# Reordering the last image's inner points, and halving one output's copy and add, in a two-layer convolution kernel

## The chip, the cores and the metric

The kernel runs on one NeuronCore of a Trainium2 chip. The metric is device time in microseconds; the runs of the kernel before gave 274.39, 275.0 and 276.09 us.

## What is computed

A batch of 16 images of 128 channels and 32 x 32 pixels passes through two residual layers. Each normalises in groups of four channels and convolves with 3 x 3 taps. The first layer mixes four expert kernels per image with a routing weight; the second uses the signs of its weights.

```python
pooled = jnp.mean(x, axis=(2, 3))
routing = jax.nn.sigmoid(pooled @ w_route.T + b_route)
y = conv(x, w_experts)                         # four experts, 3 x 3, pad 1
out = jnp.einsum('beohw,be->bohw', y, routing)
out = silu(out * inv + shift)                  # batch norm's scale and offset
...
x = x + _L0_conv_ref(_gn(x), ...)
x = x + _L1_conv_ref(_gn(x), W)                # conv with sign(W), 3 x 3, pad 1
```

## The kernel before

All 16 images stay in SBUF in the tile X, one column block of 1024 pixels each (128 channels on the partitions). The five engines run one hand-written instruction list each, and semaphores order them against one another; each engine's list is strictly in order. A loop over t runs from 1 to 16: in round t TensorE (PE) multiplies the first layer of image t in a transformed (Winograd) form, where rows are taken in tiles of four and each tile becomes six points (M1, M2, P1, P2, P0, PINF), and then the second layer of image t - 1 directly, as nine taps in two parts. The input is split into hi and lo, both f16, since the signs are exact in f16; so a half image (16 rows, one PSUM bank of pc) takes 9 products with hi and 9 with lo (sign_half, L569).

The second layer's output of an image goes from pc through ScalarE (ACT, evacuate, L945) into ev, and GpSimd (POOL, add_output, L430) adds it by a DMA that accumulates in DRAM, onto the first layer's output which SyncE (SP) has stored there (L403). POOL also takes the reciprocal root of each variance (power, L421).

The last image, 15, has no round after it, so its second layer is done in another way, behind the loop. Its first 24 rows go through the six points with f16 hi and lo parts; its last 8 rows are direct products (last_direct, L628). The names, in the order of each engine's list:

- VectorE (DVE): residual_last (L1254) adds the first layer, centre_last, last_rows_of_points (L1296, L1300), last_transform (L1308 and L1309 for the inner points M1 to P2, L1312 for the end points P0 and PINF; each raises last_v_ready, up to 5), last_low_parts (L1323 three times, for the pairs M1 and M2, P1 and P2, P0 and PINF; L1327 for the last rows), last_inverse (sums, L1336, to X, L1354) and last_outputs (L1363 twice, for the rows that P0 and PINF give).
- ACT: last_mean, last_variance (L749 to L760), variance (L808), last_hi (L923 three times, L925 for the last rows; the third waits for last_v_ready 5), evacuate of image 14 (L945), last_copy_minus (L931, which copies the bank pb into minus), last_direct_out (L936, with its own store, L939).
- PE: behind image 14's hi products come its lo products, among them the last image's residual (L617) and group variance (L494); then sign_conv_last, in this order: last_pair for pb with hi and lo, for pa with hi and lo (L606), last_direct with hi and lo (L628), last_pair for pe_ with hi and lo. A hi part waits for last_hi_ready, a lo part for last_lo_ready.
- SP: the store of the last image's 24 rows (L406) waits for both of DVE's L1363; then SP waits for the stores (stored) and for the adds (out_added).

last_inverse waits for pa (last_m_ready 2) and for ACT's minus. The three pairs each have one PSUM bank, pb, pa and pe_. The order of sign_conv_last and of ACT's tail is:

```python
for n in range(2):
    last_pair(0, n)
    last_pair(1, n)
last_direct(0)
...
last_hi()
evacuate(B - 2)
last_copy_minus()
last_direct_out()
```

Of the kernel before, what the change touches and what calls it, by code (L numbers as in the profile page):

```python
# [10 lines left out]
ALU = mybir.AluOpType  # L11
# [3 lines left out]
E, K = 4, 3  # L15
HW = H * W
# [47 lines left out]
def build(nc, x, w_experts, w_sign, params, out):  # L64
# [6 lines left out]
    with ExitStack() as ctx:  # L71
# [175 lines left out]
        h_stored = [sem(f"h_stored{i}") for i in range(B - LATE)]  # L247
        out_added = [sem("out_added0"), sem("out_added1")]
        out_ready = sem("out_ready")
        stored = sem("stored")  # L250
# [113 lines left out]


        def columns_to(c):

            return sum(cols(k)[1] - cols(k)[0] for k in range(1, c + 1))
# [12 lines left out]
        def _(sp):  # L381
# [26 lines left out]
            for p in range(2):  # L408
                sp.wait_ge(out_added[p], 16 * ((B - LATE + 1 - p) // 2))

        @block.gpsimd
        def _(pool):
# [14 lines left out]
            def add_output(i):  # L427
                pool.wait_ge(h_stored[i], 16)
                pool.wait_ge(evacuated, i + 1)
                g.dma_start(out_v[i, :, :], ev[i % 2][:], accum_op=ALU.add).then_inc(out_added[i % 2], 16)  # L430

            g.memset(nhalf[:], -0.5).then_inc(zeroed, 1)
            g.memset(ones16[:], 1.0).then_inc(zeroed, 1)
# [17 lines left out]
            for t in range(1, B + 1):  # L451
                power(t + LAG - 1)
                if 0 <= t - 2 < B - LATE:
                    add_output(t - 2)
                if ND <= t < B and t not in DVE_RESIDUAL:
                    residual(t)

        @block.tensor
        def _(pe):
# [125 lines left out]
            def last_pair(part, n):  # L585

                r = rank(B)
                bank, points = ((pb, (M1, M2)), (pa, (P1, P2)), (pe_, (P0, PINF)))[n]  # L590
                if part == 0:
                    pe.wait_ge(last_hi_ready, n + 1)
                    if n == 0:
                        pe.wait_ge(sign_points_ready, 4)
                        pe.wait_ge(minus_ready, r)
                    elif n == 1:
                        pe.wait_ge(sums_ready, 2 * r)
                    else:
                        pe.wait_ge(y_ready, 4 * r + 2)
                else:  # L600
                    pe.wait_ge(last_lo_ready, n + 1)
                for j, k in enumerate(points):
                    weights = ws[:, (k - P0) * 2 * KCO:((k - P0) * 2 + 1) * KCO] if k >= P0 else wpoint[:, k, :]
                    for m, kx in enumerate(KX_ORDER):
                        c0, c1 = reach(kx, 0, W, W)
                        mm = mm_(bank[:, 0:LAST_TILES, j, c0:c1], weights[:, kx * C:(kx + 1) * C],  # L606
                                 last_points((hi, lo)[part])[:, :, k, c0 + kx - 1:c1 + kx - 1],
                                 start=(part == j == m == 0), stop=(part == j == 1 and m == K - 1))
                if part == 1:
                    mm.then_inc(last_m_ready, 1)  # L610

# [22 lines left out]
            def sign_conv_last():  # L634
                for n in range(2):
                    last_pair(0, n)
                    last_pair(1, n)
                last_direct(0)
                last_direct(1)
                last_pair(0, 2)  # L640
                last_pair(1, 2)

# [27 lines left out]
            for t in range(1, B + 1):  # L670
# [13 lines left out]
                elif t == B - 1:  # L684
# [7 lines left out]
                    sign_half(t - 1, 1, 0, TAP_ORDER[5:])  # L692
                    sign_half(t - 1, 1, 1)
                else:
# [8 lines left out]
        def _(act):  # L703
# [38 lines left out]
            def last_variance():  # L742
# [3 lines left out]
                for half in range(2):  # L746
# [4 lines left out]
                               accum_out=(var[:, c, MID:MID + 1], last_var[:])[half]).then_inc(var_mid_ready, 1)  # L751
                    if half == 0:
                        squares(c)
                        act.wait_ge(dev2_ready, c)
                        act.wait_ge(var_mid_ready, i + 1)
                        activation(last_spread[:], dev2[:, c, MID:MID + 1], ACT.Identity, bias=var[:, c, MID:MID + 1],
                                   scale=float(HW)).then_inc(last_spread_ready, 1)
                act.wait_ge(last_spread_ready, 1)
# [182 lines left out]
            def evacuate(i):  # L941
# [3 lines left out]
                activation(ev[i % 2][:], flat(pc[:]), ACT.Copy, scale=1.0 / ACT_SCALE).then_inc(evacuated, 1)  # L945

            for q in (1, 3):
                act.dma_start(quarter(q), x_quarters[0, q, :, :]).then_inc(x_quarter_loaded[q], 16)
# [75 lines left out]
            last_hi()  # L1024
            evacuate(B - 2)
            last_copy_minus()
            last_direct_out()

        @block.vector
        def _(dve):  # L1030
# [271 lines left out]

            def last_transform():
                er, fr, vi = e_rows[:, 0:LAST_TILES], f_rows[:, 0:LAST_TILES], V[0][:, 0:LAST_TILES]
                dve.wait_ge(last_e_ready, 1)
                dve.wait_ge(last_f_ready, 1)
                for k, op, scale in ((M1, ALU.subtract, -2.0), (P1, ALU.add, 2.0)):
                    v.tensor_tensor(vi[:, :, k, :], er[:, :, 2, :], er[:, :, 1, :], op).then_inc(last_v_ready, 1)  # L1308
                    v.scalar_tensor_tensor(out=vi[:, :, k + 1, :], in0=fr[:, :, 0, :], scalar=scale,  # L1309
                                           in1=fr[:, :, 1, :], op0=ALU.mult, op1=ALU.add).then_inc(last_v_ready, 1)  # L1310
                ew = er.rearrange("p t k w -> p t (k w)")
# [3 lines left out]
            def last_low_parts():  # L1315
                c = CHAINS - 1
                dve.wait_ge(rstd_ready, c + 1)

                dve.wait_ge(sign_points_ready, 4)
                for n, k in enumerate((M1, P1, P0)):  # L1320
                    dve.wait_ge(last_hi_ready, n + 1)
                    dve.wait_ge(last_v_ready, (2, 4, 5)[n])
                    v.scalar_tensor_tensor(out=last_points(lo)[:, :, k:k + 2, :], in0=V[0][:, 0:LAST_TILES, k:k + 2, :],  # L1323
                                           scalar=rstd[:, c, MID:MID + 1], in1=last_points(hi)[:, :, k:k + 2, :],
                                           op0=ALU.mult, op1=ALU.subtract).then_inc(last_lo_ready, 1)
                dve.wait_ge(last_hi_ready, 4)
# [30 lines left out]
            def last_outputs():  # L1357
                dve.wait_ge(inner_added, 1)
                dve.wait_ge(last_m_ready, 4)
                rows = img(B - 1).rearrange("p (t k w) -> p t k w", k=TROWS, w=W)  # L1360
                for k, row, scale in ((0, 0, K_ZERO), (1, 3, K_INF)):
                    part = rows[:, 0:LAST_TILES, row, :]
                    v.scalar_tensor_tensor(out=part, in0=pe_[:, 0:LAST_TILES, k, :],  # L1363
                                           scalar=scale * INVERSE_SCALE / LAST_SCALE, in1=part,
# [100 lines left out]
```

## Time and profile before

| what | us |
|---|---|
| runs: lowest, median, highest | 274.39, 275.0, 276.09 |
| span of the profiled execution, first to last instruction | 276.8 |
| PE busy | 267.2 |
| DVE busy | 255.8 |
| ACT busy | 219.8 |
| POOL busy | 54.4 |

Of the profiled execution the span is what the profile gives; it is 1.8 us longer than the median of the runs. Times in the rows are microseconds from the start of the span. A line of a timeline or of a chain gives the start, the duration, the engine, the line of the kernel and the operation, what it writes and reads, and how many instructions are merged (x9); in brackets stands how long the engine was idle before it and who ended that. The ends of PE's products are modelled, and a product's record overlaps the next one's; the distance of two starts is the better price.

### The profile page before, as it was taken

What the parts mean: (1) busy time and instruction counts of PE and PEld (TensorE: products, weight loads), DVE (VectorE), ACT (ScalarE), POOL (GpSimd) and SP (SyncE); (2) the same over time, 40 slices, a digit from 0 to 9 for tenths busy, and PEclk for the clock granted to TensorE, in tenths of its full rate; (3) what the DMA queues carried; (4) which work ended last, traced back from release to release, by engine and by line L of the source; (5) the groups of instructions that cost most, each with busy time, mean ns of one, the idle gap of its engine ahead of it and who ended that gap; (6) DMA issues with size and microseconds to landing.
All of it is one profiled execution on the core that took longest, in us unless ns stands there. A gap on an engine that the chain in (4) does not pass through costs nothing.

```text
span 276.8 us, 4115 instructions
## 1 busy us (share of the span) xinstructions
PE 267.2 (97%) x1336; PEld 183.2 (66%) x1336; DVE 255.8 (92%) x466; ACT 219.8 (79%) x450; POOL 54.4 (20%) x63
## 2 busy tenths in 40 slices
PE   7699989999999999999999999999999999999993
PEld 7444764857667584857667584857667584857663
DVE  5679979999999999999999999999999999996885
ACT  2458789897979989798989989798989987745870
POOL 3001011311203141311303141311314141210110
PEclk9779999999999999999999999999999999999999
DMA  7988953163554536264454436254554437273507
GB/s 216 394 316 290 322 182 76 78 114 114 78 153 60 99 91 127 82 97 134 76 152 62 94 88 129 89 94 133 78 153 57 95 90 133 85 123 107 76 2 152
DMA packets 11253, 35.20 MB, mean 127 GB/s; under 512 B 1248, under 2 KB 3424, under 8 KB 11232
## 3 DMA queue, kind: packets, MB, share of 16 engines
q0 software_dynamic: 4176, 15.21, 33.0%
q1 hardware_dynamic: 6624, 19.34, 18.9%
q10 hardware_dynamic: 432, 0.39, 0.4%
q8 instruction: 11, 0.18, 0.3%
q14 instruction: 10, 0.08, 0.1%
HBM read 11.34 MB, written 16.25 MB: 100 GB/s over the span
## 4 chain that ended last, share of the span: by engine, by line
PE 91%; DMA 3%; DVE 2%; ACT 1%; issue 1%; SPq 1%; POOL 0%; DVEq 0%; ACTq 0%
PE pc L569 41%; PE pa L534 14%; PE pb L534 14%; PE pe_ L534 13%; PE pd L524 6%; DMA we<-w_experts 3%; PE ps L504 1%; PE ps L508 1%; DVE U L1129 0%; PE pa L606 0%; POOL rstd L421 0%; PE pb L606 0%; DVE X L1354 0%; ACT hi L906 0%; SPq L389 0%
## 5 line engine op out<-in xcount | busy, mean ns | idle before, releaser
L1139 DVE SCALAR_TENSOR_TENSOR U<-we,route,U 128x1152 f32<-128x1152 f32 x45 | 63.6, 1413 | 0.6
L569 PE MATMUL pc<-hi,ws 128*128 128x496 f16 (+3 forms) x270 | 59.8, 375 | 0.8 <-ACT hi L906 0.8
L569 PE MATMUL pc<-lo,ws 128*128 128x496 f16 (+3 forms) x270 | 59.7, 375 | 0.0
L421 POOL TENSOR_TENSOR rstd<-ve,nhalf 128x2 f32<-128x2 f32 (+1 forms) x19 | 26.7, 1407 | 139.4 <-ACT ve L821 113.2
L569 PEld LDWEIGHTS pc<-hi,ws 128*128 128x128 f16 x270 | 26.4, 98 | 30.3 <-issue 1.2
L569 PEld LDWEIGHTS pc<-lo,ws 128*128 128x128 f16 x270 | 26.5, 102 | 27.8
L534 PE MATMUL pa<-V,UM 128*128 128x256 f32 (+1 forms) x180 | 41.7, 381 | 0.0
L534 PE MATMUL pb<-V,UM 128*128 128x256 f32 (+1 forms) x180 | 40.7, 376 | 0.1
L534 PE MATMUL pe_<-V,U 128*128 128x256 f32 (+1 forms) x180 | 40.6, 375 | 0.0
L534 PEld LDWEIGHTS pb<-V,UM 128*128 128x128 f32 x180 | 34.1, 190 | 5.4 <-issue 0.6
L534 PEld LDWEIGHTS pe_<-V,U 128*128 128x128 f32 x180 | 34.1, 190 | 3.8
L534 PEld LDWEIGHTS pa<-V,UM 128*128 128x128 f32 x180 | 33.1, 190 | 3.3
L425 POOL DMA_DIRECT2D X<-y x14 | 12.4, 883 | 65.6 <-ACT y L891 65.6
L729 ACT ACTIVATE junk_mid<-X,stats 128x1024 f32<-128x1024 f32 x15 | 17.2, 1148 | 9.4 <-DMA X<-y 9.4
L906 ACT ACTIVATE hi<-X,nbias,rstd 128x1024 f16<-128x1024 f32 (+2 forms) x16 | 18.9, 1187 | 0.5
L863 ACT ACTIVATE U<-we,route 128x1152 f32<-128x1152 f32 x15 | 18.8, 1256 | 0.5
L845 ACT ACTIVATE xn<-X,nbias,rstd 128x1024 f32<-128x1024 f32 (+1 forms) x16 | 19.2, 1200 | 0.0
L524 PE MATMUL pd<-xn,U 128*128 128x496 f32 (+3 forms) x36 | 18.2, 653 | 0.3 <-DVE U L1129 0.3
L913 ACT ACTIVATE hn<-X,nbias,rstd 128x1024 f32<-128x1024 f32 x15 | 18.4, 1229 | 0.0
L1261 DVE TENSOR_TENSOR lo<-hn,hi 128x1024 f16<-128x1024 f32 x15 | 18.3, 1221 | 0.0
L1170 DVE SCALAR_TENSOR_TENSOR e_rows<-xn 128x1024 f32<-128x1024 f32 x15 | 18.2, 1216 | 0.0
L891 ACT ACTIVATE y<-y,bn_shift,bn_tiles 128x1024 f32<-128x1024 f32 x14 | 17.2, 1230 | 1.2 <-DVE y L1240 1.2
(165 smaller groups left out, 396.1 us busy)
## 6 DMA issues: line engine op xcount, KB each, us to landing
X<-x SPq DMA_DIRECT2D x15, 512.0 KB, 5.1
out<-X SPq DMA_DIRECT2D x15, 512.0 KB, 2.6
out<-ev POOLq DMA_DIRECT2D x15, 512.0 KB, 5.5
X<-y POOLq DMA_DIRECT2D x14, 512.0 KB, 4.5
we<-w_experts SPq DMA_DIRECT2D x3, 768.0 KB, 10.0
ws_raw<-w_sign SPq DMA_DIRECT2D x1, 576.0 KB, 12.5
out<-X SPq DMA_DIRECT2D x1, 384.0 KB, 2.8
X<-x SPq DMA_DIRECT2D x2, 128.0 KB, 2.8
```

What stands on the lines that cost most here:

```text
L421: g.tensor_tensor(rstd[:, c, a:b], ve[:, c, a:b], nhalf[:, a:b], ALU.pow).then_inc(rstd_ready, 1)
L524: mm = mm_(rows[:, r0 - half * (H // 2):r1 - half * (H // 2), c0:c1], U[i % RING][:, slot, kx * C:(kx + 1) * C], xn[i % RING][:, r0 + ky:r ...
L534: mm = mm_(bank[:, :, j, c0:c1], weights[:, kx * C:(kx + 1) * C], V[t % 2][:, :, k, c0 + kx - 1:c1 + kx - 1], start=(n == 0), stop=(n == K ...
L569: mm = mm_(rows[:, r0 - first // W:r1 - first // W, c0:c1], ws[:, tap * C:(tap + 1) * C], plane((hi, lo)[part], i)[:, r0 + ky - 1:r1 + ky ...
L729: activation(junk["mid"][:], img(i), ACT.Square, bias=nm(c, MID), accum_out=var[:, c, MID:MID + 1]).then_inc(var_mid_ready, 1)
L845: activation(xn[i % RING][:, 1 + first:1 + last, :], img(i).rearrange("p (h w) -> p h w", h=H)[:, first:last, :], ACT.Identity, bias=nbias ...
L863: activation(flat(U[i % RING][:]), flat(we[:, 0, :, :]), ACT.Copy, scale=route[:, i, 0:1]).then_inc(mix_first, 1)
L906: activation(plane(hi, i)[:, first:last, :], img(i).rearrange("p (h w) -> p h w", h=H)[:, first:last, :], ACT.Identity, bias=nbias[:, c, M ...
L913: activation(hn[:], img(i), ACT.Identity, bias=nbias[:, c, MID:MID + 1], scale=rstd[:, c, MID:MID + 1]).then_inc(hn_ready, 1)
L1139: v.scalar_tensor_tensor(out=flat(U[i % RING][:]), in0=flat(we[:, e, :, :]), scalar=route[:, i, e:e + 1], in1=flat(U[i % RING][:]), op0=AL ...
L1170: v.scalar_tensor_tensor(out=flat3(e_rows[:]), in0=flat(xn[i % RING][:, 0:H, :]), scalar=-4.0, in1=flat(xn[i % RING][:, 2:2 + H, :]), op0= ...
L1261: v.tensor_tensor(lo[i % 2][:, 0:HW], hn[:], hi[i % 2][:, 0:HW], ALU.subtract).then_inc(lo_ready, 1)
```

## The change

Image 14's lo products of the second half are split: four taps stay, two go between the hi and lo parts of the first inner pair (pb), and three go behind the second inner pair (pa). The end points come last as before, but in a function of their own (last_ends) that does P0 with hi and lo and then PINF with hi and lo, PINF into the unused half of pd, so that DVE's last_outputs has a wait for each.

On DVE the transform and the low parts are cut up: inner points, low part of M1 and M2, low part of P1 and P2, end points, low part of P0 and PINF, low part of the last rows. On ACT the squares and the spread of the last variance come behind both halves' squares instead of between them; the evacuation of image 14 is done in halves, the first ahead of last_copy_minus, the second behind it. POOL adds each half with a DMA of its own, behind its loop; SP waits for both. last_hi on ACT is as before.

```diff
@@ sync
-                sp.wait_ge(out_added[p], 16 * ((B - LATE + 1 - p) // 2))
+                sp.wait_ge(out_added[p], 16 * ((B - LATE - p) // 2))
+                sp.wait_ge(half_added[p], 16)
@@ gpsimd
+            def add_output_half(i, half):
+                part = slice(half * BANK, (half + 1) * BANK)
+                pool.wait_ge(h_stored[i], 16)
+                pool.wait_ge(evacuated, i + half + 1)
+                g.dma_start(out_v[i, :, part], ev[i % 2][:, part], accum_op=ALU.add).then_inc(half_added[half], 16)
...
-                if 0 <= t - 2 < B - LATE:
+                if 0 <= t - 2 < B - LATE - 1:
                     add_output(t - 2)
...
+            for half in range(2):
+                add_output_half(B - 2, half)
@@ tensor
+            def last_ends():
+                r = rank(B)
+                pe.wait_ge(last_hi_ready, 3)
+                pe.wait_ge(y_ready, 4 * r + 2)
+                pe.wait_ge(silu_ready, 1)
+                for j, k in enumerate((P0, PINF)):
+                    weights = ws[:, j * 2 * KCO:(j * 2 + 1) * KCO]
+                    for part in range(2):
+                        if j == 0 and part == 1:
+                            pe.wait_ge(last_lo_ready, 3)
+                        for m, kx in enumerate(KX_ORDER):
+                            c0, c1 = reach(kx, 0, W, W)
+                            mm = mm_(last_end(j)[:, :, c0:c1], weights[:, kx * C:(kx + 1) * C],
+                                     last_points((hi, lo)[part])[:, :, k, c0 + kx - 1:c1 + kx - 1],
+                                     start=(part == m == 0), stop=(part == 1 and m == K - 1))
+                    mm.then_inc(last_m_ready, 1)
...
             def sign_conv_last():
-                for n in range(2):
-                    last_pair(0, n)
-                    last_pair(1, n)
+                i = B - 2
+                last_pair(0, 0)
+                sign_half(i, 1, 1, TAP_ORDER[4:6])
+                last_pair(1, 0)
+                last_pair(0, 1)
+                last_pair(1, 1)
+                sign_half(i, 1, 1, TAP_ORDER[6:])
                 last_direct(0)
                 last_direct(1)
-                last_pair(0, 2)
-                last_pair(1, 2)
+                last_ends()
...
-                    sign_half(t - 1, 1, 1)
+                    sign_half(t - 1, 1, 1, TAP_ORDER[:4])
@@ scalar
-                    if half == 0:
-                        squares(c)
...
+                squares(c)
+                act.wait_ge(dev2_ready, c)
+                act.wait_ge(var_mid_ready, i + 1)
+                activation(last_spread[:], dev2[:, c, MID:MID + 1], ACT.Identity, bias=var[:, c, MID:MID + 1],
+                           scale=float(HW)).then_inc(last_spread_ready, 1)
...
+            def evacuate_half(i, half):
+                act.wait_ge(conv_ready, 2 * i + half + 1)
+                act.wait_ge(out_added[i % 2], 16 * (i // 2))
+                activation(ev[i % 2][:, half * BANK:(half + 1) * BANK], pc[:, half, :], ACT.Copy,
+                           scale=1.0 / ACT_SCALE).then_inc(evacuated, 1)
...
             last_hi()
-            evacuate(B - 2)
+            evacuate_half(B - 2, 0)
             last_copy_minus()
+            evacuate_half(B - 2, 1)
             last_direct_out()
@@ vector
-                dve.wait_ge(last_m_ready, 4)
...
                 for k, row, scale in ((0, 0, K_ZERO), (1, 3, K_INF)):
+                    dve.wait_ge(last_m_ready, 4 + k)
...
-                    v.scalar_tensor_tensor(out=part, in0=pe_[:, 0:LAST_TILES, k, :],
+                    v.scalar_tensor_tensor(out=part, in0=last_end(k),
...
-            last_transform()
-            last_low_parts()
+            last_transform_pairs()
+            last_low_pair(0)
+            last_low_pair(1)
+            last_transform_ends()
+            last_low_pair(2)
+            last_low_rest()
             last_inverse()
             last_outputs()
```

## Rows read from the trace of the kernel before

**Rows 1.** The page's first part: span, and busy time of an engine
```profile
span 276.8 us, 4115 instructions
PE 267.2 (97%) x1336; PEld 183.2 (66%) x1336; DVE 255.8 (92%) x466; ACT 219.8 (79%) x450; POOL 54.4 (20%) x63
```

**Rows 2.** The chain that ended last, its end: start, us, what
```profile
269.84 0.56 DVE sums L1336
...
272.96 0.36 DVE X L1363
```

**Rows 3.** Timeline of PE from 264.6: start, us, line, operation
```profile
264.83 2.92 PE L569 MATMUL pc<-lo,ws 128*128 128x465 f16 x13
267.58 0.66 PE L606 MATMUL pb<-hi,wpoint 128*128 128x192 f16 x6
...
269.07 0.66 PE L606 MATMUL pa<-lo,wpoint 128*128 128x192 f16 x6
269.57 1.11 PE L628 MATMUL pd<-hi,ws 128*128 128x256 f16 x9
...
271.46 0.66 PE L606 MATMUL pe_<-hi,ws 128*128 128x192 f16 x6
271.96 0.66 PE L606 MATMUL pe_<-lo,ws 128*128 128x192 f16 x6
```

**Rows 4.** Timeline of ACT from 264.9
```profile
266.16 1.62 ACT L923 ACTIVATE hi<-V,rstd 128x384 f16<-128x384 f32 x3 [0.89 <-POOL rstd L421]
267.69 0.52 ACT L925 ACTIVATE hi<-xn,rstd 128x288 f16<-128x288 f32 x1
268.11 1.00 ACT L945 ACTIVATE ev<-pc 128x1024 f32<-128x1024 f32 x1
269.02 0.47 ACT L931 ACTIVATE minus<-pb 128x384 f32<-128x384 f32 x1
```

**Rows 5.** Timeline of DVE from 266.1
```profile
266.15 0.55 DVE L1312 TENSOR_TENSOR V<-e_rows 128x384 f32<-128x384 f32 x1
266.98 1.68 DVE L1323 SCALAR_TENSOR_TENSOR lo<-V,rstd,hi 128x384 f16<-128x384 f32 x3 [0.28 <-ACT hi L923]
268.57 0.51 DVE L1327 SCALAR_TENSOR_TENSOR lo<-xn,rstd,hi 128x288 f16<-128x288 f32 x1
...
272.96 0.62 DVE L1363 SCALAR_TENSOR_TENSOR X<-pe_,X 128x192 f32<-128x192 f32 x2
```

**Rows 6.** Timeline of POOL, its last two adds and the root between them
```profile
256.88 0.89 POOL L430 DMA_DIRECT2D out<-ev  x1 [1.30 <-ACT ev L945]
265.36 0.76 POOL L421 TENSOR_TENSOR rstd<-ve,nhalf 128x1 f32<-128x1 f32 x1 [7.59 <-ACT ve L808]
269.66 0.89 POOL L430 DMA_DIRECT2D out<-ev  x1 [3.53 <-ACT ev L945]
```

**Rows 7.** SyncE's waits from 260 (us in total, times, longest), and its last store
```profile
SPq L71 <- DMA out<-X: 1.2, 1, 1.2
SPq L409 <- DMA out<-ev: 1.2, 1, 1.2
...
273.61 0.33 SPq L406 DMA_DIRECT2D out<-X  x1
```

**Rows 8.** The page's DMA issues: KB each, us from issue to landing
```profile
out<-X SPq DMA_DIRECT2D x15, 512.0 KB, 2.6
out<-ev POOLq DMA_DIRECT2D x15, 512.0 KB, 5.5
...
out<-X SPq DMA_DIRECT2D x1, 384.0 KB, 2.8
```

**Rows 9.** ACT's groups by shape: copies out of PSUM, busy us, mean ns
```profile
L945 ACT ACTIVATE ev<-pc 128x1024 f32<-128x1024 f32 x15 | 15.5, 1031 | 0.0
...
L880 ACT ACTIVATE minus<-pb 128x512 f32<-128x512 f32 x15 | 8.9, 595 | 0.0
```

**Rows 10.** DMA from 256.8 to 263.0: busy tenths in 40 slices of 0.155 us
```profile
DMA  0000000004900009597996999999996000000000
```

More of the change, by code:

```diff
@@ L248, in build @@
         out_added = [sem("out_added0"), sem("out_added1")]
+        half_added = [sem("half_added0"), sem("half_added1")]
         out_ready = sem("out_ready")
@@ L363, in last_rest, with last_end @@
             return part[(B - 1) % 2][:, n:n + LAST_REST * W].rearrange("p (h w) -> p h w", w=W)
+        def last_end(j):
+            bank = flat3(pe_[:]) if j == 0 else pd[:, 1, :]
+            return bank[:, 0:LAST_TILES * W].rearrange("p (t w) -> p t w", w=W)
         def columns_to(c):
@@ L589, in last_pair @@
                 r = rank(B)
-                bank, points = ((pb, (M1, M2)), (pa, (P1, P2)), (pe_, (P0, PINF)))[n]
+                bank, points = ((pb, (M1, M2)), (pa, (P1, P2)))[n]
                 if part == 0:
@@ L595, in last_pair @@
                         pe.wait_ge(minus_ready, r)
-                    elif n == 1:
+                    else:
                         pe.wait_ge(sums_ready, 2 * r)
-                    else:
-                        pe.wait_ge(y_ready, 4 * r + 2)
                 else:
@@ L602, in last_pair @@
                 for j, k in enumerate(points):
-                    weights = ws[:, (k - P0) * 2 * KCO:((k - P0) * 2 + 1) * KCO] if k >= P0 else wpoint[:, k, :]
                     for m, kx in enumerate(KX_ORDER):
                         c0, c1 = reach(kx, 0, W, W)
-                        mm = mm_(bank[:, 0:LAST_TILES, j, c0:c1], weights[:, kx * C:(kx + 1) * C],
+                        mm = mm_(bank[:, 0:LAST_TILES, j, c0:c1], wpoint[:, k, kx * C:(kx + 1) * C],
                                  last_points((hi, lo)[part])[:, :, k, c0 + kx - 1:c1 + kx - 1],
@@ L751, in last_variance @@
                                accum_out=(var[:, c, MID:MID + 1], last_var[:])[half]).then_inc(var_mid_ready, 1)
-                    if half == 0:
-                        squares(c)
[L754 to L757, printed above, removed]
+                squares(c)
[3 more added lines that the diff above has]
+                           scale=float(HW)).then_inc(last_spread_ready, 1)
                 act.wait_ge(last_spread_ready, 1)
@@ L1301, in last_rows_of_points, with last_transform_pairs @@
                                 rows(0)[:, :, W:3 * W], ALU.subtract).then_inc(last_f_ready, 1)
-            def last_transform():
+            def last_transform_pairs():
                 er, fr, vi = e_rows[:, 0:LAST_TILES], f_rows[:, 0:LAST_TILES], V[0][:, 0:LAST_TILES]
@@ L1310, in last_transform, with last_transform_ends @@
                                            in1=fr[:, :, 1, :], op0=ALU.mult, op1=ALU.add).then_inc(last_v_ready, 1)
+            def last_transform_ends():
+                er, vi = e_rows[:, 0:LAST_TILES], V[0][:, 0:LAST_TILES]
                 ew = er.rearrange("p t k w -> p t (k w)")
@@ L1313, in last_transform, with last_low_pair, last_low_rest @@
                                 ew[:, :, 2 * W:4 * W], ew[:, :, 0:2 * W], ALU.subtract).then_inc(last_v_ready, 1)
-            def last_low_parts():
-                c = CHAINS - 1
+            def last_low_pair(n):
+                c, k = CHAINS - 1, (M1, P1, P0)[n]
                 dve.wait_ge(rstd_ready, c + 1)
                 dve.wait_ge(sign_points_ready, 4)
[L1320 to L1325, printed above, removed]
+                dve.wait_ge(last_hi_ready, n + 1)
+                dve.wait_ge(last_v_ready, (2, 4, 5)[n])
+                v.scalar_tensor_tensor(out=last_points(lo)[:, :, k:k + 2, :], in0=V[0][:, 0:LAST_TILES, k:k + 2, :],
+                                       scalar=rstd[:, c, MID:MID + 1], in1=last_points(hi)[:, :, k:k + 2, :],
+                                       op0=ALU.mult, op1=ALU.subtract).then_inc(last_lo_ready, 1)
+            def last_low_rest():
+                c = CHAINS - 1
                 dve.wait_ge(last_hi_ready, 4)
```

## The prediction

> **What bounds the kernel now.** I read the page first: TensorE is busy for 267.2 of the 276.8 us of the span [rows 1], so nearly everything up to the last image is set by PE's own queue, and the change leaves that part alone. It only reorders work after about 262 us. So the second view is the chain that ended last, of the last 15 us [rows 2]: PE runs without a gap through image 14's products and the inner pairs of the last image (pb, pa), and from there VectorE carries the end: the sums at 269.84, and the last writes into X from 272.96. The third view is the timeline of each engine over that stretch [rows 3, 4, 5, 6], read for what each queue does next. The last is SyncE's waits and the DMA landings [rows 7, 8]: SP waits 1.2 us for image 14's added output, and after it another 1.2 us for the store of the last image, so the store is what ends the span. It is issued at 273.61 and lands 2.8 us later, 276.41; the span closes 0.4 us behind that. Hence what moves the end is the moment at which DVE finishes X, 273.58 (272.96 + 0.62 [rows 5]), and, some 1.2 us of slack behind it, image 14's add (issued 269.66, landing 5.5 later: 275.2).
>
> What starts DVE's last chain? Its sums need three things: pa (PE, last pair issued at 269.07 and ended 269.73 [rows 3]), minus (ACT, 269.02 + 0.47 = 269.49 [rows 4]) and DVE itself being through with its low parts (268.57 + 0.51 = 269.08 [rows 5]). Today pa is last, with ACT only 0.24 us ahead of it.
>
> **PE's part of the change.** Thirteen products of image 14 take from 264.83 to 267.58 [rows 3], 2.75/13 = 0.212 us each. Eight now stand ahead of the first pair, two between its hi and lo parts, three behind pa. PE reaches the first pair at 264.83 + 8 x 0.212 = 266.52. But that pair needs ACT's first hi: it starts at 266.16 behind POOL's rstd (265.36 + 0.76 = 266.12 [rows 6]) and takes 0.60 (three in 1.62 us [rows 4], started 0.51 apart), so to 266.76. DVE, which waits for the same hi, starts at 266.98 [rows 5]; I take a value between, 266.92, so PE stands for 0.40 us. From there: pb hi 0.50 us (four groups of six from 267.58 to 269.57 [rows 3]), two products 0.42, pb lo, pa hi and pa lo 0.50 each: the last group starts at 268.84 instead of 269.07. Five products fewer ahead of pa would be 1.06 us; two still lie ahead, which takes 0.42 off, and the stall 0.40: pa is earlier by only 0.23 us. Behind it PE does the three products (0.64), the direct rows (0.94 + 0.95 [rows 3]) and the end points, and is through with issuing at 268.84 + 0.50 + 0.64 + 1.89 + 1.0 = 272.87, against 272.46 now. That 0.4 us costs nothing as long as DVE comes to the end points later than that; it does, below.
>
> **DVE's and ACT's part.** The transform of the end points (0.55 us at 266.15) now runs in time in which DVE would else wait for ACT's first hi: its idle time ahead of 266.98 is 0.28 us [rows 5]. The change puts it behind the second low part. The low parts gain nothing by that: the first waits for the first hi in either order, so it starts at 266.98 and the second 0.54 later (three in 1.68), and the transform runs from 268.05 to 268.60 instead of from 266.15 to 266.70. But ACT's third hi waits for that transform (last_v_ready 5), and that function is as before: ACT's queue is in order, so it stands from 267.28, when its second hi is done, to about 268.65. Behind it on ACT are the third hi (to 269.25), the rest's hi (0.52, to 269.68), now the copy of half an output, and only then minus. Starts on ACT follow each other 0.09 us inside the previous record (267.69 + 0.52 against 268.11 [rows 4]). The half copy of 512 columns is priced by the rows of 512 and 1024 columns out of PSUM, 0.60 and 1.03 us [rows 9]; I take 0.58: it runs from 269.58 to 270.15. Minus starts at 270.06 and ends at 270.53, where it ended at 269.49. With the 0.22 us from hi's end to DVE's start, the sums start at 270.75 instead of 269.84: **0.91 us later**. Halving the copy gives back 0.4 us of what the queue lost (a whole copy ahead would have been 1.03); the copy of the other half stands behind minus and needs conv_ready, at 270.1.
>
> Bounds of this term: with no hand-over time at all minus would be at hand at 270.45. But DVE itself isn't free before: its third low part waits for the third hi (269.25 + 0.22), takes 0.54, and the rest's low part 0.48 to the next start, so 270.49, or +0.65. With 0.2 us at each of the two hand-overs (DVE to ACT, ACT to DVE) it is +1.1. So +0.65 to +1.1, and I take 0.9.
>
> From the sums to the end of X DVE has the same instructions: 3.74 us [rows 2, 5], so 274.49. The two reads of the end points now lie in two banks and have a wait each; since DVE comes to them at 273.87 and PE issued its last group's end well before (272.87, with a fill of 0.2), both waits are met and the split is worth nothing. Without that cover it would save at most one group, 0.5 us. The store is issued at 274.52 and lands 2.8 later [rows 8] at 277.3.
>
> **The variance's reorder.** ACT's squares and spread move behind the second half's square. The same five instructions follow one another, the last one starting at about 264.2 as before; PE's group variance is issued behind the residual product and waits for it in either order. Zero, give or take 0.1, which would shift everything behind it alike.
>
> **The halved add.** POOL issues behind ACT's copy with 0.55 us of hand-over (269.11 to 269.66 [rows 4, 6]) and 0.89 an issue. Half 0: copy ended 270.15, issued 270.70. Half 1: copy from 270.44 to 271.0, issued 271.55 to 271.6. How long half an add takes no row shows. Whole ones land in 5.5 us [rows 8]; in the add that ran alone, issued at 256.88 [rows 6], the engines' busy stretch lies at 259.1 to 261.6 (slices 15 to 30 of 0.155 us [rows 10]), so 2.2 us ahead of the data, 2.5 of data, the rest completion. If data goes by bytes, half 1 moves from about 274.0 to 275.6 and lands at 276; if it goes by rows (as many rows, half as long), the two halves take 2.5 to 3.1 each behind one another from 273.0, to 278 or 279.2, and land with 0.3 more. SP's plain stores don't settle it, since of their landing little is data: 512 KB took 2.6 us and 384 KB 2.8 [rows 8]. I take nearer to the bytes, since with 16 engines busy through the whole stretch it is more likely the data than the count that fills it: half 1 lands between 276 and 277, under the store's 277.3. The Trainium skill (DMA: Bandwidth & Descriptors, Anatomy of one DMA) speaks against such a split: a DMA from GpSimd has about 2.0 us that doesn't scale, and only the rest goes by bytes at 436 GB/s. By it half an add would be an estimated 0.6 us shorter than a whole, landing at 276.5; no row here shows halves, and the sum stands without it.
>
> **Sum.** The end goes from 276.41 + 0.4 to 277.3 + 0.4 = 277.7 in the profiled execution, +0.9 us on 276.8. The median of the runs shown is 275.0, 1.8 below that execution; the same 0.9 on it gives **275.9**.
>
> **The rivals.**
> A, the forecast: ACT's queue is held by the late transform; +0.65 to +1.1, 275.6 to 276.1.
> B, faster: PE's pa stays what the sums wait for, and its 0.23 us is gained: 274.8. It decides if minus is at hand by 269.5, which takes a third hi that starts no later than about 267.6. For it speaks that pa is last today; against it that the third hi can't start ahead of the transform's end, which is at 268.6 by the order on DVE. If the first hi came 0.4 us sooner, B would be worth 0.6.
> C, slower still: the halves' adds go by rows and end the span. Half 1 at 278.3 to 279.5 instead of the store's 277.3 gives +1.9 to +3.1: 276.9 to 278.1. It decides once half an add lands more than 5.7 us after its issue at 271.6. For it: the DMA engines are already busy nearly throughout while one add moves [rows 10]; the store would share the engines with it. Against it: the traffic is the same in bytes.
> D, nothing to see: gains and losses under 0.3 us, because another instruction on ACT gives way (say the hand-overs are shorter than I took): 275.0.
>
> **How the numbers follow.** A 0.65, B 0.08, C 0.15, D 0.12. The runs of before spread from 274.39 to 276.09, so a median may sit half a microsecond off any case. The range reaches from B and D's lower side to the lower part of C: 274.6 to 277.2; A's own is 275.3 to 276.5. About 1%, 2.75 us, is what a measurement of this kernel can tell from no change. Over 1% slower needs the upper end of C, 277.75: 0.05. Over 1% faster has no case, 0.02 for what I don't see. The rest, 0.93, is within 1%.
>
> **What would show it.** PE idle for some 0.4 us ahead of its first pair, released by ACT's hi; ACT idle for some 1.4 us ahead of the third hi, released by DVE's last transform; DVE's sums released by ACT's minus at about 270.75 instead of by pa; the last X at 274.5; SP's last wait still for the store. The forecast is wrong if the sums start before 269.9, or if SP's last long wait is for the second half's add.

## The result

The changed kernel takes 276.41 us (median of 22 runs, 275.24 to 279.9), the kernel before 275.0 beside it. The ratio, from which the slow executions of both kernels are left out, is 1.0045 (95% interval 1.0028 to 1.0063), some 1.2 us slower; the medians of all runs differ by 1.4. The forecast was 275.9, 0.9 us slower.

The two profiled executions can't be compared by their spans, 276.8 and 274.9: the one of before ran the second and third of its 40 slices at a lower granted clock (digit 7, a mix of TensorE's 1.2 and 2.4 GHz levels), the one of after at 2.4 GHz throughout (9 tenths or more in every slice), which the page's second part shows (before, then after):

```profile
PEclk9779999999999999999999999999999999999999
```
```profile
PEclk9999999999999999999999999999999999999999
```

A run's time lies 1.8 us above its span (276.73 for the 274.9), so the 276.8 of before belongs to an execution some 3.6 us above the median of 275.0, not 1.8; the forecast only adds a difference to that median, so its number doesn't hang on this. All tails below are measured from one instruction that is the same in every kernel, PE's last group mean, which starts at 262.14 in the profile before and at 258.44 in the one after (timeline of PE, two products each). The profiles of e3, e7, e8 and e11 dip in the same two slices, ahead of the mean and so outside every tail.

```profile
262.14 0.38 PE L485 MATMUL ps<-stats,gmat 128*128 128x1 f32 x2
```
```profile
258.44 0.38 PE L500 MATMUL ps<-stats,gmat 128*128 128x1 f32 x2
```

After it, the timelines of the changed kernel read (start, us, line, tile; in brackets the idle time before and who ended it), first PE's products ahead of the first pair, that pair's hi part and pa's last group, then ACT, then DVE, then POOL and SP:

```profile
261.24 1.88 PE L584 MATMUL pc<-lo,ws 128*128 128x465 f16 x8
263.13 0.67 PE L618 MATMUL pb<-hi,wpoint 128*128 128x192 f16 x6
...
265.06 0.66 PE L618 MATMUL pa<-lo,wpoint 128*128 128x192 f16 x6
```
```profile
262.46 1.12 ACT L955 ACTIVATE hi<-V,rstd 128x384 f16<-128x384 f32 x2 [0.78 <-POOL rstd L428]
264.93 0.61 ACT L955 ACTIVATE hi<-V,rstd 128x384 f16<-128x384 f32 x1 [1.36 <-DVE V L1354]
265.45 0.52 ACT L957 ACTIVATE hi<-xn,rstd 128x288 f16<-128x288 f32 x1
265.88 0.57 ACT L982 ACTIVATE ev<-pc 128x512 f32<-128x512 f32 x1
266.36 0.47 ACT L963 ACTIVATE minus<-pb 128x384 f32<-128x384 f32 x1
```
```profile
263.28 1.15 DVE L1364 SCALAR_TENSOR_TENSOR lo<-V,rstd,hi 128x384 f16<-128x384 f32 x2 [0.74 <-ACT hi L955]
264.35 0.55 DVE L1354 TENSOR_TENSOR V<-e_rows 128x384 f32<-128x384 f32 x1
265.75 0.62 DVE L1364 SCALAR_TENSOR_TENSOR lo<-V,rstd,hi 128x384 f16<-128x384 f32 x1 [0.85 <-ACT hi L955]
266.28 0.51 DVE L1371 SCALAR_TENSOR_TENSOR lo<-xn,rstd,hi 128x288 f16<-128x288 f32 x1
266.86 0.56 DVE L1380 TENSOR_TENSOR sums<-pa,minus 128x384 f32<-128x384 f32 x1
...
270.26 0.35 DVE L1407 SCALAR_TENSOR_TENSOR X<-pd,X 128x192 f32<-128x192 f32 x1
```
```profile
267.00 1.79 POOL L443 DMA_DIRECT2D out<-ev  x2 [4.58 <-ACT ev L982]
```
```profile
270.64 0.33 SPq L412 DMA_DIRECT2D out<-X  x1
```

Against [rows 4], where ACT's three hi follow one another without a gap, ACT now stands 1.36 us ahead of the third, until DVE's transform of the end points (L1354) is done. Minus ends at 266.83, 8.39 us after the group mean, where it ended 7.35 after it (269.49). Against [rows 2], the sums start 8.42 instead of 7.70 us after the mean: 0.72 later, and the store is issued 12.20 instead of 11.47 after it [rows 7]. That is the forecast's mechanism, by two ways at once: the sums come 0.03 us behind minus, and 0.07 us behind DVE's own last low part (266.28 + 0.51 = 266.79), which the late third hi holds up just as much. But the store also lands later (DMA issues of the end of the span, KB each, us from issue to landing; then SP's waits in us):

```profile
out<-ev POOLq DMA_DIRECT2D x2, 256.0 KB, 4.8
out<-X SPq DMA_DIRECT2D x1, 384.0 KB, 3.7
```
```profile
SPq L416 <- DMA out<-ev: 2.4, 1, 2.4
SPq L71 <- DMA out<-X: 0.9, 1, 0.9
```

The store took 2.8 us [rows 8] and now takes 3.7. The forecast's sum had no such term.

### The profile page after: what moved, and what is told of

Read it like the earlier page. It is cut to its first block, busy times and chain, and to the rows that moved or that the text cites. A ratio compares the mean times of both kernels' runs of the same rounds, so it can differ in the third digit from the quotient of the medians.

```text
span 274.9 us, 4122 instructions
## 1 busy us (share of the span) xinstructions
PE 265.0 (96%) x1336; PEld 181.6 (66%) x1336; DVE 256.1 (93%) x466; ACT 219.9 (80%) x451; POOL 55.5 (20%) x64
## 4 chain that ended last, share of the span: by engine, by line
PE 90%; DMA 2%; DVE 2%; ACT 2%; issue 1%; POOL 1%; SPq 1%; DVEq 0%; ACTq 0%
PE pc L584 41%; PE pa L549 14%; PE pb L549 14%; PE pe_ L549 13%; PE pd L539 6%; DMA we<-w_experts 2%; PE ps L519 1%; POOL rstd L428 1%; PE ps L523 1%; DVE U L1168 0%; DVE X L1398 0%; DVE lo L1364 0%; ACT hi L938 0%; SPq L395 0%; ACT hi L955 0%
## 5 line engine op out<-in xcount | busy, mean ns | idle before, releaser
L539 PE MATMUL pd<-xn,U 128*128 128x496 f32 (+3 forms) x36 | 15.9, 586 | 1.1 <-DVE U L1168 1.1
```

What stands on the lines that cost most here:

```text
L539: mm = mm_(rows[:, r0 - half * (H // 2):r1 - half * (H // 2), c0:c1], U[i % RING][:, slot, kx * C:(kx + 1) * C], xn[i % RING][:, r0 + ky:r ...
```

## The experiments

Theory 1: ACT's queue, held up by the late transform, delays minus and the sums. Theory 2: the add of image 14 comes so late that the last store is held up by it. The rival of 2 is that two DMAs in place of one do it. Theory 3, made after e1 to e7, widens 2 to the kernel before: wherever an add is late, the last store lands 1.0 to 1.2 us after the last add has landed, and alone 2.3 us after its issue. All results, in us after PE's last group mean, each from the run's own profile; the adds' landing is issue plus the time to landing; "closes" is the end of the span; the ratio of times is against the kernel before, with its interval:

| kernel | sums | store issued | last add issued | last add landed | store takes | closes | ratio |
|---|---|---|---|---|---|---|---|
| before | 7.70 | 11.47 | 7.52 | 13.0 | 2.8 | 14.66 | |
| after | 8.42 | 12.20 | 9.46 | 15.0 | 3.7 | 16.46 | 1.0045 (1.0028 to 1.0063) |
| e1 ends early | 7.39 | 11.20 | 9.07 | 12.9 | 2.9 | 14.54 | 0.9996 (0.9963 to 1.0028) |
| e2 before, ends late | 8.85 | 12.62 | 8.99 | 14.3 | 2.9 | 15.92 | 1.0051 (1.0014 to 1.0088) |
| e3 no add of 14 | 8.42 | 12.19 | none | | 2.3 | 14.92 | 1.0001 (0.9966 to 1.0035) |
| e4 before, halves | 7.70 | 11.47 | 8.16 | 13.0 | 2.8 | 14.64 | 0.9993 (0.9960 to 1.0026) |
| e5 one add | 8.43 | 12.20 | 9.18 | 15.0 | 4.0 | 16.67 | 1.0125 (1.0081 to 1.0168) |
| e6 hi hi lo lo | 7.09 | 10.90 | 8.77 | 13.7 | 3.8 | 15.16 | 1.0007 (0.9979 to 1.0036) |
| e7 variance back | 8.43 | 12.20 | 9.4 | 14.8 | 3.6 | 16.35 | one execution |
| e8 half first | 7.70 | 11.47 | 8.16 | 12.0 | 2.3 | 14.18 | 0.9967 (0.9928 to 1.0005) |
| e9 before, no add of 14 | 7.70 | 11.47 | none | | 2.3 | 14.18 | 0.9969 (0.9933 to 1.0006) |
| e10 before, late add | 7.70 | 11.48 | 9.56 | 15.9 | 5.3 | 17.32 | 1.0093 (1.0056 to 1.0131) |
| e11 both | 7.17 | 10.98 | 8.85 | 12.9 | 3.2 | 14.53 | 0.9993 (0.9973 to 1.0013) |

**e1: DVE's order alone undone.**

```diff
             last_transform_pairs()
+            last_transform_ends()
             last_low_pair(0)
             last_low_pair(1)
-            last_transform_ends()
             last_low_pair(2)
```

> The changed kernel with one thing undone: DVE does the transform of the end points ahead of the first low part again. Theory 1 (ACT's queue, held by that transform, delays minus and with it DVE's sums): the 1.4 us gap ahead of ACT's third hi goes, the sums start 7.4 to 7.8 us after PE's last group mean (before 7.7, changed 8.4), and the time falls by 0.7 to 1.2 us, to 275.1 to 275.6. Theory 2 (the halved add, which runs beside the last store, carries the loss): the sums come earlier but the store still lands 3.5 us or more after its issue and the time stays at 276.0 or above.

ACT's gap is gone, minus is copied 1.5 us sooner, and the sums wait for pa again (timelines of ACT and DVE):

```profile
262.48 1.62 ACT L955 ACTIVATE hi<-V,rstd 128x384 f16<-128x384 f32 x3 [0.77 <-POOL rstd L428]
...
264.91 0.47 ACT L963 ACTIVATE minus<-pb 128x384 f32<-128x384 f32 x1
```
```profile
265.85 0.56 DVE L1380 TENSOR_TENSOR sums<-pa,minus 128x384 f32<-128x384 f32 x1 [0.44 <-PE pa L618]
```

The sums start 7.39 us after the mean, 1.03 sooner than in the changed kernel and 0.31 sooner than before: PE's reorder does give the sums what it promises, once ACT isn't held. The time is that of the kernel before (the interval allows 0.28%, 0.8 us, above it) and the span closes 0.12 us sooner, so undoing this one order takes the loss away. It takes away both its parts, since ACT's queue held the halves' copies as well as minus: the store took 2.9 us, which theory 2 as I had put it did not expect; the half copied first was added 1.5 us earlier here, and its packets were nearly through when the second one's began.

**e2: the kernel before with DVE's order alone changed.**

```diff
                 for n, k in enumerate((M1, P1, P0)):
+                    if n == 2:
+                        last_transform_ends()
                     dve.wait_ge(last_hi_ready, n + 1)
...
-            last_transform()
+            last_transform_pairs()
             last_low_parts()
```

last_transform is cut into two functions for it, with the same instructions.

> The kernel before with only DVE's order changed: the transform of the end points stands behind the second low part. Theory 1: ACT idles about 1.4 us ahead of the third hi, and here a whole copy of image 14 stands ahead of minus, so the sums start about 1.4 us later than before (9.1 after PE's last group mean) and the time rises by 1.2 to 1.6 us, to 276.2 to 276.6. Rival: DVE's order is harmless, the sums stay at 7.7 and the time at 275.0 to 275.3.

ACT stands 1.36 us ahead of its third hi here too, and DVE's sums wait for minus:

```profile
264.37 0.61 ACT L923 ACTIVATE hi<-V,rstd 128x384 f16<-128x384 f32 x1 [1.36 <-DVE V L1315]
```
```profile
266.73 0.56 DVE L1341 TENSOR_TENSOR sums<-pa,minus 128x384 f32<-128x384 f32 x1 [0.67 <-ACT minus L931]
```

DVE's own low parts are through at 266.06 here. Minus ends at 266.70, so the hand-over from ACT takes 0.03 us. The sums are 1.15 us later than before, a little less than expected, and the ratio 1.0051 is 1.4 us. The loss follows the order on DVE without PE's change. The ACT copy ahead of minus is a whole one here, and it stands behind the same gap, so the add is late as well (issued 8.99, 1.47 later than before), about as much as the store (1.15).

**e3 and e9: no add of image 14, in the changed kernel and in the kernel before.**

```diff
-            for half in range(2):
-                add_output_half(B - 2, half)
...
-                sp.wait_ge(half_added[p], 16)
```

That is e3, in which both halves are still copied. e9 ends POOL's loop of adds one image earlier, and SP waits for one add less:

```diff
-                if 0 <= t - 2 < B - LATE:
+                if 0 <= t - 2 < B - LATE - 1:
                     add_output(t - 2)
```

> The changed kernel without image 14's add (both halves are copied but not added, so that image lacks its second layer). Theory 2 (the store of the last image shares the DMA engines with the halves' adds): the store lands 2.5 to 2.9 us after its issue instead of 3.7, and the time falls by 0.7 to 1.0 us to 275.4 to 275.7. Rival: the store's 3.7 us come from its own queue or from ACT's small store beside it; it stays at 3.5 to 3.9 and the time at 276.2 to 276.5.

> The kernel before without image 14's add (that image lacks its second layer). Theory 3: also in the kernel before it is the add that holds up the store, so the store lands in 2.2 to 2.4 us instead of 2.8 and the time falls by 0.4 to 0.6 us. Rival (in the kernel before the add is out of the store's way): 2.7 to 2.9 us, and no difference in time.

Without the add the store lands 2.3 us after its issue in both (DMA issues, the same line in e3 and e9):

```profile
out<-X SPq DMA_DIRECT2D x1, 384.0 KB, 2.3
```

So in the changed kernel the add costs the store 1.4 us, and in the kernel before 0.5. Theory 3's 2.2 to 2.4 (e9) holds; theory 2's 2.5 to 2.9 (e3) was too high, and its rival's 3.5 to 3.9 is out. ACT's small store (128 KB) takes 1.7 us in both, against 3.4 in the kernel before and 4.9 in the changed one, so the add holds that one up too. With no add in either, the changed kernel's span closes 0.74 us later (14.92 against 14.18): that is DVE's chain alone, and the other 1.06 of the 1.80 between the two kernels comes only with the add. In time, e3 falls to that of the kernel before, a little more than the 0.7 to 1.0 us expected; e9's ratio 0.9969 has an interval that reaches to 1.0006, so its half microsecond is shown by the trace and only likely by the clock.

**e4: the kernel before with copy and add in halves alone.**

```diff
             last_hi()
-            evacuate(B - 2)
+            evacuate_half(B - 2, 0)
             last_copy_minus()
+            evacuate_half(B - 2, 1)
```

POOL adds each half with a DMA of its own and SP waits for both, as in the changed kernel.

> The kernel before with only image 14's copy and add in halves, the first half copied ahead of minus, the second behind it. If a halved add goes by bytes (theory 2 needs only that it comes late): adds issued at about 269.2 and 270.1 on the clock of the profile before, done by 275.5, the store lands in 2.8 to 3.2 us, and the time is 274.8 to 275.4. Rival: two DMAs cost a fixed part or go by rows, the adds end after 276.5 and the time is 275.8 or more.

The adds are issued 7.09 and 8.16 after the mean, the last lands at 13.0 as the whole one did, the store takes 2.8 us. Halving costs nothing and brings nothing here that the time can tell (ratio 0.9993).

**e5: the changed kernel with one add behind both half copies.**

```diff
-            for half in range(2):
-                add_output_half(B - 2, half)
+            pool.wait_ge(evacuated, B)
+            add_output(B - 2)
```

SP waits for that one add, as in the kernel before.

> The changed kernel with both half copies, but one whole add of image 14 behind them instead of two of halves. Theory 2a (it is the lateness of the adds against the store, not their number): the one add is issued 9.4 us after PE's last group mean, lands 5.3 to 5.6 us later at 14.8 (changed: second half at 15.0), the store still lands 3.4 to 3.9 us after its issue, and the time is that of the changed kernel within 0.3 us. Theory 2b (two DMAs in place of one are what fills the engines): the add ends by 14.3, the store lands in 2.8 to 3.1 us and the time falls by 0.6 us or more, to 275.8 or below.

The one add lands at 15.0, when the second half did, and the store takes 4.0 us:

```profile
out<-X SPq DMA_DIRECT2D x1, 384.0 KB, 4.0
```

So it isn't the number of DMAs. The time is not the changed kernel's within 0.3 us, as was expected: 1.0125 is 3.4 us, while the span closes only 2.0 later than before. The profiled execution, 276.15 us, is the fastest of the six; what else moved in the others it doesn't show.

**e10: the kernel before with POOL's add held back, all else in its order.**

```diff
                 pool.wait_ge(evacuated, i + 1)
+                if i == B - 2:
+                    pool.wait_ge(last_rows_ready, 1)
                 g.dma_start(out_v[i, :, :], ev[i % 2][:], accum_op=ALU.add).then_inc(out_added[i % 2], 16)
```

> The kernel before, but POOL issues image 14's add only after DVE's third instruction of the last inverse, some 1.5 us later; DVE's chain and the store's issue (11.47 after PE's last group mean) stay. Theory 3: the add lands 1.3 to 1.7 us later than in the kernel before (at 14.4 to 14.8 after the mean), the store lands 1.0 to 1.2 us behind it, 4.0 to 4.4 us after its issue, and the time rises by 1.2 to 1.6 us, to 276.0 to 276.4, with no change in any engine's order. Rival (the engines share by bytes only, and the store's 384 KB lose at most half their rate): the store lands in 3.3 us or less, and the add ends last; time up by 0.5 to 0.9.

The add is issued 2.04 us later than before and the span closes 2.66 later; the time rises by 0.93%, 2.6 us. DVE, ACT and PE are where they were; the store is issued at 11.48 and takes 5.3 us instead of 2.8. Theory 3 has the direction, but every size came out larger than it said (1.5 us for the add, 4.0 to 4.4 for the store, 1.2 to 1.6 for the time). The DMA queues show why the store is late (packets, MB, share of 16 engines; q0 is POOL's queue with the add, q1 SP's with the store, issued at 269.76). The issue of the store, then the queues from 270 to 271, from 272 to 273, and from 273 to 274:

```profile
out<-X SPq DMA_DIRECT2D x1, 384.0 KB, 5.3
```
```profile
q0 software_dynamic: 8, 0.03, 37.7%
```
```profile
q0 software_dynamic: 54, 0.22, 110.7%
```
```profile
q1 hardware_dynamic: 83, 0.25, 64.2%
q0 software_dynamic: 29, 0.05, 29.1%
```

For more than 3 us after its issue not one packet of the store moves; from 270 to 273 q0 is alone. The view counts a packet's whole time where it starts, which gives shares above 100% and, from 270 to 271, one that looks small; by the start and duration of each packet in the trace, 16 or more packets of the add, as many as there are engines, are at work at every moment from 269.7 to 273.2. In e9, where no add is about, the store (issued 269.39) has moved 103 packets between 269.4 and 271:

```profile
q1 hardware_dynamic: 103, 0.32, 50.0%
```

So the store gets no engine until the add that is there first is nearly through. It isn't ACT's small store that is in its way: that one's packets ended at 269.57. In the changed kernel the two do share for a while at the end: from 272 to 272.5 the store moved 15 packets beside 30 of the adds'. In the ten kernels whose last add lands at 12.9 or later the store lands 0.9 to 1.3 us after it, issued 1.5 to 4.4 us before that landing; in e8, where it lands at 12.0, the store takes the 2.3 us that it takes alone.

**e7: the variance's order put back in the changed kernel.**

```diff
-                squares(c)
-                act.wait_ge(dev2_ready, c)
...
+                    if half == 0:
+                        squares(c)
+                        act.wait_ge(dev2_ready, c)
...
```

> The changed kernel with the order of squares and spread in the last variance put back. If that reorder is what made PE wait 0.1 us at the last group variance, PE's products of image 14 resume 2.69 us after the last group mean as before, instead of 2.80, and all that follows comes 0.1 us earlier: sums at 8.3. Rival: it makes no difference, 2.80 and 8.4. The time is not to be told from 276.4 in one look.

PE's products resume 2.69 us after the mean, where the changed kernel has 2.80, but the sums stay at 8.43: ACT's first hi starts 4.02 after the mean in both, as before. The reorder costs PE 0.11 us, as expected, but nothing was waiting for it, so the expected 0.1 us behind it did not come.

**e8, e6 and e11: versions meant to be better.** In e8 the first half's copy stands ahead of the last image's hi parts, in ACT's wait for the root:

```diff
+            evacuate_half(B - 2, 0)
             last_hi()
-            evacuate(B - 2)
             last_copy_minus()
+            evacuate_half(B - 2, 1)
```

The rest is the kernel before, with POOL and SP as in e4.

> The kernel before with image 14's copy and add in halves, and the first half copied ahead of the last image's hi parts, in ACT's wait for the root. Theory 3 (the store of the last image lands 1.0 to 1.2 us after the last add has landed, and alone in 2.3): the first half's add is issued about 4.9 us after PE's last group mean and is over before the store; the second is issued at 7.4 and lands at 11.3 to 11.9, at about the store's issue (11.47). The store lands in 2.3 to 2.6 us, and the time is 0.3 to 0.5 us below the kernel before. Rival: ACT's copy delays hi, and with it the pairs or the sums, by more than the store gains; sums after 7.9 and a time of 275.0 or more.

The first half's add is issued 4.88 after the mean, the copy delays ACT's first hi by 0.2 us, which the sums don't feel (7.70), and the last half is issued at 8.16 (7.4 was expected) and lands at 12.0. The store takes 2.3 us and the span closes 0.48 us sooner than before (DMA issues):

```profile
out<-ev POOLq DMA_DIRECT2D x2, 256.0 KB, 3.8
out<-X SPq DMA_DIRECT2D x1, 384.0 KB, 2.3
```

The ratio 0.9967 is the best of all, with an interval up to 1.0005: likely faster than the kernel before, not settled.

e6 takes the changed kernel, puts DVE's and the variance's order back, and does the pairs as pb hi, pa hi, pb lo, pa lo behind ten products, so that PE has no wait in between:

```diff
                 last_pair(0, 0)
-                sign_half(i, 1, 1, TAP_ORDER[4:6])
+                last_pair(0, 1)
                 last_pair(1, 0)
-                last_pair(0, 1)
                 last_pair(1, 1)
...
-                    sign_half(t - 1, 1, 1, TAP_ORDER[:4])
+                    sign_half(t - 1, 1, 1, TAP_ORDER[:6])
```

> A version meant to be better than both: the changed kernel with DVE's order and the variance's order of the kernel before, ten instead of eight products ahead of the pairs, and the pairs as pb hi, pa hi, pb lo, pa lo, so that PE needn't wait for ACT's first hi. Theory 1 (the sums wait for the latest of pa, minus and DVE's low parts): pa is through 6.9 to 7.1 us after the last group mean, the sums start at 7.05 to 7.25 (before 7.7), the store is issued at 10.8 to 11.0, half 1's add is issued at 8.8 and lands beside the store. With a store of 2.8 to 3.1 us the tail is 0.3 to 0.6 us shorter than before: 274.3 to 274.6. If the late half takes the store's engines as in the changed kernel (3.7 us), nothing is left: 274.9 to 275.3.

> The version with the pairs as pb hi, pa hi, pb lo, pa lo behind ten products (and DVE's and the variance's order of the kernel before), and on top of it the first half's copy ahead of the last image's hi parts. Theories 1 and 3 together: the sums start about 7.1 to 7.2 us after PE's last group mean and the store is issued at 10.9 to 11.0; half 0's add is issued at 4.9 and is out of the way, half 1's at 8.8 and lands at 12.3 to 12.7, so the store lands at 13.3 to 13.8 and the span closes 0.4 us behind, 13.7 to 14.2 (kernel before 14.66, changed kernel 16.46). The time is 0.5 to 0.9 us below the kernel before. Rival: the late second half takes the store as long as in the version without the early copy (3.8 us), and the span closes at 15.1, 0.4 us behind the kernel before.

In e6 the sums start 0.61 us sooner than before and the store is issued 0.57 sooner, and nothing comes of it: the last half's add lands at 13.7, the store lands 1.0 behind it, 3.8 us after its issue, and the span closes 0.50 later than before. e11 adds the early copy of e8. Its sums and its store come 0.5 sooner than before, but the last half is issued at 8.85, lands at 12.9, and the store takes 3.2 us: the span closes at 14.53, between the two expectations. Neither time can be told from that of the kernel before.

## Why the prediction was right, and where its sum was off

**The queue on ACT: right.** A gap of 1.37 us ahead of the third hi was forecast, 1.36 measured; minus was to end 8.39 us after the mean (270.53) and did. e1 and e2 show that this order makes the loss in either surrounding.

**The sums: 0.91 forecast, 0.72 measured.** The mis-sized term is the hand-over from ACT to DVE; the 0.72 lies inside the term's bounds of 0.65 to 1.1, near the lower one, which is DVE's own low parts. I took 0.22 us, from the end of hi to the start of the low part [rows 5]; from minus to the sums it is 0.03. The chain of after shows where the 0.22 goes, in DVE's queue between the end of ACT's hi (263.08) and the low part: two steps of its wait lines (L1362, L1363) and the short stretches of issue between them:

```profile
263.08 0.03 issue
263.11 0.02 DVEq L1362
263.13 0.05 issue
263.18 0.05 DVEq L1363
263.23 0.06 issue
263.28 0.35 DVE lo L1364
```

**PE's part: right within 0.1.** pa's last group starts 6.62 us after the mean (forecast 268.84, so 6.70). The stall ahead of the first pair is 0.2 instead of 0.4 us: PE came 0.11 later (e7) and ACT's hand-over took 0.06, not 0.16. It decided nothing, as forecast, and neither did the end points' split.

**The variance's reorder: zero forecast, zero measured at the sums** (e7; PE alone came 0.11 us later, about the 0.1 that was allowed for).

**The halves: right that data goes by bytes.** In the profile after, q0 carries 288 packets where it had 144, in nearly the same share of the engines (48.1% of the last 7.9 us, against 44.0% of the last 7.8). Clearer is e8's first half, which moves alone: 144 packets in 1.9 us of all 16 engines (45.8% of 266.8 to 271), where the whole add that ran alone took 3.5 for as many (56.1% of 256.8 to 263). Rival C, adds by rows that land after the store, did not come true, but it was nearer than the sum had it: the second half landed 5.6 us after its issue, with C's line at 5.7 and my range at 4.4 to 5.4. Two readings of the add that ran alone were off. The engines' stretch was read from the slices in which most packets start; by the packets' own times it runs from 258.4 to 261.9, 1.5 us behind the issue and 3.5 long, not 2.2 and 2.5. And its landing comes 0.4 us or so behind its data, not the 0.8 that this reading leaves; the forecast used 0.3 to 0.4 without saying why. The estimate from the Trainium skill (DMA: Bandwidth & Descriptors, Anatomy of one DMA), half an add 0.6 us shorter than a whole, is not borne out either: e8's first half landed 3.9 us after its issue and e11's 4.1, the whole one alone 5.4.

**The store: the step that failed.** I added the store's 2.8 us as a constant and read SP's two waits [rows 7] as 1.2 us of slack behind the add. There was none: the store was already held by the add, and the 1.2 us are the distance at which it lands behind it. The prediction named the sharing of engines only under rival C, and its sum has no price for it. e9 shows 0.5 us of its 2.8 to be the add's doing, e10 that holding the add back moves the end by more than as much (2.04 and 2.66). In the changed kernel the last half is issued 1.94 us later than the whole add was, the store 0.73 later, and the store's term becomes 3.7. By its own steps the sum should have read +0.72 and +0.9.

So one error was 0.19 too much and the other 0.9 too little. The measured 1.24 lies above the +1.1 that the forecast gave as its own upper bound, and inside its wider range. The tail of the profile closes 1.80 us later than before, while the times differ by 1.24 (0.77 to 1.73); the last add's landing differs between profiles of the same tail order (15.0 in after, 14.8 in e7), and how much of the rest is that scatter stays open. The forecast of 0.9 lies inside the interval, but through a sum that lacked a term as large as the one it had; that it came so near is in part luck.

Four runs moved the end by about half a microsecond or more without moving DVE's chain, e3 from the changed kernel and e8, e9 and e10 from the kernel before. They say that image 14's add is on the path beside DVE's sums. Leaving the add out (e3) and putting the order back (e1) each bring the time back to that of the kernel before, but not by the same way: e1 undoes both parts, while e3 removes the add's part and work with it, and keeps the 0.72 us on DVE (sums at 8.42).

## What to carry to other kernels

When a step is moved behind another on one in-order queue, ask what a second engine's in-order queue has behind the instruction that waits for it: here 0.55 us of transform, moved out of DVE's idle time, held ACT for 1.36 us. And do not read two waits in a row at the end of a kernel as slack of the first: in every run here a store that was issued while an accumulating DMA had still to move its data landed behind it, so the add's issue time belongs into the sum. What was free here was the copy of an already finished half, in a wait that ACT has anyway.

## What was not expected of the hardware

A store of 384 KB on SP's queue took 2.3 us alone and up to 5.3 us with an add on POOL's queue ahead of it, and in e10 moved nothing from 270 to 273, while 0.39 MB of the add's 0.52 moved. The Trainium skill (DMA: Bandwidth & Descriptors, Queues, rings and completion order) states that an increment of a semaphore lands only after every earlier write of that DMA engine, across its queues; the landings behind one another agree with that. But the same page (SWDGE vs HWDGE vs iDMA) has each engine go round-robin between its queues, and by that a store whose descriptors are there would move beside the add. The trace differs, and decides: in e10 95 packets of the add started between 270 and 273 and none of the store, whose packets came when q0's were nearly through. ACT's small store (128 KB) did move beside the adds in the changed kernel, taking 4.9 us where it took 3.4 before and 1.7 with no add, so it is not that an add shuts all other queues out. Whether the store's descriptors or its data waited, no run here tells apart; if its descriptors came that late, the page's rule could still hold.
